# Expert phase: channel norm in 32x32 blocks turned by DVE, two batches ahead, in place of sixteen TensorE transpositions

## What is computed

```
out  = Wout @ attention(...) + b_out[:, None]            # per batch, 128 x 1024
mean = out.mean(axis=channels); var = out.var(axis=channels)
o    = (out - mean) * rsqrt(var + 1e-5) * g[:, None]     # channel norm: one mean, one variance per column n
x    = x + o
xf   = layernorm(x)                                      # over the 1024 columns of a row
scores = xf @ Wr.T                                       # 64 experts; top 16, softmax -> G
h    = xf @ A                                            # 64 x 16 = 1024 hidden values per row
x    = x + 2 * ((h * G) @ B)
```

## Time and profile before

| | |
|---|---|
| median of 3 runs | 2001.52 us (1999.25 to 2002.13) |
| profiled execution, its own time | 2002.66 us |
| its span in the profile | 2000.9 us |
| mean granted clock of TensorE | 0.99 |
| PE busy | 1920.2 us (96%), 10780 products |
| weight loads on PE | 1662.5 us (83%) |
| DVE busy | 1381.6 us (69%) |
| ACT busy | 1038.8 us (52%) |
| POOL busy | 803.9 us (40%) |
| DMA | 127.64 MB, mean 64 GB/s |

### The profile page before, as it was taken

How to read it: one execution, slowest core, us unless ns; L and a number is a source line. 1 busy time by engine, 2 the same in 40 slices (tenths; PEclk the granted TensorE clock), 3 DMA queues, 4 the chain that set the end, 5 groups by cost and what they waited for, 6 DMA issues and landing times. The chain is left out here.

```text
span 2000.9 us, 29856 instructions
## 1 busy us (share of the span) xinstructions
PE 1920.2 (96%) x10780; PEld 1662.5 (83%) x10780; DVE 1381.6 (69%) x1985; ACT 1038.8 (52%) x1303; POOL 803.9 (40%) x456
## 2 busy tenths in 40 slices
PE   4999999999999999999998699999999999999999
PEld 3778888888888888888886589999999999999998
DVE  5988888888888888888885654544444454444443
ACT  3888878787878787878785611111111111111111
POOL 3767676767676767667674000000000000000000
PEclk9999999999999999999999799999999999999999
DMA  3121111111111111212111611111111111111110
GB/s 117 44 72 61 68 63 63 63 63 63 63 63 65 61 73 52 73 52 73 52 43 37 213 61 64 63 57 46 54 63 63 63 63 63 63 63 51 44 41 32
DMA packets 43999, 127.64 MB, mean 64 GB/s; under 512 B 4224, under 2 KB 14080, under 8 KB 43968
## 3 DMA queue, kind: packets, MB, share of 16 engines
q1 hardware_dynamic: 39360, 110.44, 15.9%
q0 software_dynamic: 4608, 16.78, 2.7%
HBM read 93.65 MB, written 33.55 MB: 64 GB/s over the span
## 5 line engine op out<-in xcount | busy, mean ns | idle before, releaser
L282 POOL TENSOR_TENSOR kT_lo<-kT,kT_hi 128x1024 fp32r<-128x1024 f32 x128 | 304.4, 2399 | 0.6 <-ACT kT_hi L324 0.5
L278 POOL TENSOR_TENSOR eq<-eq,q_inv 128x1024 f32<-128x1024 f32 x128 | 242.4, 1904 | 140.6 <-DVE q_inv L499 140.6
L961 POOL TENSOR_TENSOR rstd_c<-var_c,minus_half 128x8 f32<-128x8 f32 x32 | 52.7, 1648 | 549.7 <-DVE var_c L1100 549.7
L52 PE MATMUL ps<-w_ra_hi,xT_hi 128*128 128x384 f32 (+1 forms) x768 | 257.9, 336 | 0.0
L54 PE MATMUL ps<-w_ra_hi,xT_lo 128*128 128x384 f32 (+1 forms) x768 | 252.2, 328 | 0.0
L53 PE MATMUL ps<-w_ra_lo,xT_hi 128*128 128x384 f32 (+1 forms) x768 | 251.9, 328 | 0.0
L983 ACT CAST hT_hi<-ps 128x512 fp32r<-128x512 f32 x64 | 37.7, 589 | 376.0 <-PE ps L1157 376.0
L52 PE MATMUL ps<-w_b_hi,hT_hi 128*128 128x512 f32 x512 | 205.7, 402 | 0.0
L342 ACT ACTIVATE ek<-ps,k_min 128x1024 f32<-128x1024 f32 x128 | 142.4, 1112 | 119.7 <-DVE k_min L503 119.7
L54 PE MATMUL ps<-w_b_hi,hT_lo 128*128 128x512 f32 x512 | 201.0, 393 | 0.0
L53 PE MATMUL ps<-w_b_lo,hT_hi 128*128 128x512 f32 x512 | 200.6, 392 | 0.0
(11 more groups left out here) (142 smaller groups left out, 4576.4 us busy)
## 6 DMA issues: line engine op xcount, KB each, us to landing
x_sb<-in_x SPq DMA_DIRECT2D x64, 512.0 KB, 4.1
ctx_sb<-in_ctx SPq DMA_DIRECT2D x32, 512.0 KB, 3.3
ctx_hi<-in_ctx POOLq DMA_DIRECT2D x32, 512.0 KB, 3.7
attention_out<-o_sb SPq DMA_DIRECT2D x32, 512.0 KB, 2.6
o_sb<-attention_out SPq DMA_DIRECT2D x32, 512.0 KB, 3.9
out<-out_sb SPq DMA_DIRECT2D x32, 512.0 KB, 2.9
x<-in_L_ffn_A SPq DMA_DIRECT2D x2, 512.0 KB, 4.0
o_sb<-in_L_ffn_A SPq DMA_DIRECT2D x2, 512.0 KB, 3.6
```

The lines of the kernel that those rows point to most:

```text
L52: pe.matmul(out, stat_hi, mov_hi, start=first, stop=False)
L278: pool.tensor_tensor(v, v, per_row(q_inv[:, i, :], 2 * HEADS, DH), ALU.mult).then_inc(q_normed, 1)
L282: pool.tensor_tensor(kT_lo[:, i % 2, :, :], kT[:, i % 2, :, :], kT_hi[:, i % 2, :, :].bitcast(F32), ALU.subtract).then_inc(kT_lo_ready, 1)
```

## The change

Steps now begin at t = -2, and the channel norm is made for batch u = t + 2 (`early`), in a different way:

- DVE turns o in 32x32 blocks from `o_sb` to `o_blk` (one instruction over 128x1024). In each block the 32 columns of o stand on partitions then, and the 32 channels along the row; the four bands of 32 partitions hold the four parts of the channels.
- ACT squares `o_blk` into PSUM slot 0, DVE sums each block's row of 32 (128x32 sums, `sq_part`).
- PE adds the four bands with one product of 32 columns by a constant matrix `row_mean` (1/128 where two partitions are alike modulo 32).
- DVE adds eps, POOL takes the power over 128x32, and then POOL, not DVE, multiplies `o_blk` in place by it.
- DVE turns the blocks back into `o_sb`. x2 reads it from there a step later.

PE's two turns of 8 transpositions each go, and hidden group 1 runs in one piece. The raw buffer that was half of `o_sb` is now `hg`; the loads of o are made two steps ahead of their use in x2; weight jobs are spread over steps -2, -1 and 0. On DVE the second block turn stands before the gating of the last hidden group, and on POOL the power for x2's rows stands before that for the channels. Cut to its core:

```diff
-            return {(-1, "var"): range(0, 2), (-1, "o"): range(2, 4), (-1, "y"): range(4, 6),
-                    (-1, "norm"): range(6, 7), (-1, "x"): range(7, A_JOBS),
+            return {(-2, "o"): range(0, 3), (-2, "y"): range(3, 5), (-1, "o"): range(5, 6),
+                    (-1, "y"): range(6, 7), (-1, "norm"): range(7, 8), (-1, "x"): range(8, A_JOBS),
 # SP
-                wait_for(sp, o_turned, b - 1)
+            def load_o(u, p):
+                wait_for(sp, x2_ready, u - 1)
+                sp.dma_start(o_sb[:, p, :], o_dram[u]).then_inc(o_loaded[p], 16)
-                    if n == 2:
-                        sp.wait_ge(o_stored[1], 16 * BATCHES // 2)
+                if not isinstance(t, int) or 0 < t + 2 < BATCHES:
+                    load_x(t + 2, par)
+                if not isinstance(t, int) or 1 < t + 3 < BATCHES:
+                    load_o(t + 3, 1 - par)
+            sp.wait_ge(o_stored[1], 16 * BATCHES // 2)
+            load_o(1, 1)
             load_weights()
 # POOL
                     pool.tensor_tensor(rstd[:, :], veps[:, :], w["minus_half"][:, :], ALU.pow).then_inc(rstd_ready, 1)
+                if early:
+                    pool.wait_ge(var_ready, u + 1)
+                    pool.tensor_tensor(rstd_c[:, :], var_c[:, :], w["minus_half"][:, 0:1].broadcast_to([P, NBLK]),
+                                       ALU.pow).then_inc(rstd_c_ready, 1)
+                    pool.wait_ge(rstd_c_ready, u + 1)
+                    v = o_blk[:, :].rearrange("p (n c) -> p n c", c=BLK)
+                    pool.tensor_tensor(v, v, per_row(rstd_c[:, :], NBLK, BLK), ALU.mult).then_inc(y_blocked, 1)
 # ACT
-                    act.activation(work[:, :], OT.rearrange(flat), ACT.Square).then_inc(squared, 1)
+                if early:
+                    act.wait_ge(o_blocked, u + 1)
+                    wait_for(act, x_lo_ready, u - 1)
+                    act.activation(SQ.rearrange(flat), o_blk[:, :], ACT.Square).then_inc(squared, 1)
 # DVE
+                if early:
+                    dve.wait_ge(o_loaded[par], 8 * (u - par) + 16)
+                    wait_for(dve, y_ready, u)
+                    dve.transpose(o_blk[:, :], o_sb[:, par, :]).then_inc(o_blocked, 1)
+                    dve.wait_ge(squared, u + 1)
+                    dve.tensor_reduce(sq_part[:, :], SQ.rearrange("p a (n c) -> p (a n) c", c=BLK), X,
+                                      ALU.add).then_inc(sq_summed, 1)
                 if mix:
                     top_scores(t)
                     gates(t)
                     gate_hidden(t, 0)
 ...
+                if early:
+                    dve.wait_ge(var_made, u + 1)
+                    dve.tensor_scalar(var_c[:, :], VAR, EPS, None, ALU.add).then_inc(var_ready, 1)
+                if mix:
+                    gate_hidden(t, 1)
 ...
                 if mix:
                     turned_hidden(t, 0)
+                if early:
+                    dve.wait_ge(y_blocked, u + 1)
+                    dve.transpose(o_sb[:, par, :], o_blk[:, :]).then_inc(y_ready, 1)
+                if mix:
                     gate_hidden(t, 2)
 # PE
-                    turn(OT.rearrange(flat), o_sb[:, p, :], o_turned)
+                if early:
+                    pe.wait_ge(sq_summed, u + 1)
+                    pe.matmul(VAR, row_mean[:, :], sq_part[:, :], start=True, stop=True).then_inc(var_made, 1)
-                    hidden(1, range(NCH // 2))
-                if ahead:
-                    pe.wait_ge(y_ready, b + 1)
-                    turn(YT.rearrange(flat), work[:, :], y_turned)
-                    hidden(1, range(NCH // 2, NCH)).then_inc(h_made, 1)
+                    hidden(1, range(NCH)).then_inc(h_made, 1)
```

More of the change, by code:

```diff
@@ L792 @@
 A_JOBS = 1 + KCH
+BLK = 32
+NBLK = N // BLK
 WEIGHT_JOBS = A_JOBS + KCH
@@ L814, in expert_mix @@
         work = sb("work", [P, N])
+        o_blk = sb("o_blk", [P, N])
+        row_mean = sb("row_mean", [P, P])
+        ident_sum = sb("ident_sum", [P, BLK])
         xT_hi = sb("xT_hi", [P, NCH, P], F32R)
@@ L836, in expert_mix @@
         gate = sb("gate", [P, EXPERTS])
-        raw = [x_sb[:, 1, :], x2[:, 1, :], o_sb[:, 1, :], out_sb[:, :]]
+        raw = [x_sb[:, 1, :], x2[:, 1, :], hg[:, :], out_sb[:, :]]
         RAW = len(raw)
@@ L893, in each_step @@
         def each_step(eng, step):
-            for t in (-1, 0, 1, 2):
-                step(t, t % 2, t >= 0, True, t >= 1)
-            with eng.Fori(0, (BATCHES - 4) // 2) as i:
+            for t in (-2, -1, 0, 1, 2):
+                step(t, t % 2, t >= 0, t >= -1, t >= 1, True)
+            with eng.Fori(0, (BATCHES - 6) // 2) as i:
                 for k in range(2):
-                    step(2 * i + 3 + k, (3 + k) % 2, True, True, True)
-            step(BATCHES - 1, (BATCHES - 1) % 2, True, False, True)
-            step(BATCHES, BATCHES % 2, False, False, True)
+                    step(2 * i + 3 + k, (3 + k) % 2, True, True, True, True)
+            for t in range(BATCHES - 3, BATCHES + 1):
+                step(t, t % 2, t < BATCHES, t < BATCHES - 1, True, t < BATCHES - 2)
         block = ctx.enter_context(nc.Block())
@@ L906, in _, with load_x @@
         def _(sp):
-            def load(b, p):
-                wait_for(sp, o_turned, b - 1)
-                if isinstance(b, int) and b == 1:
-                    sp.wait_ge(b_ordered[1], KCH // 2 - 1)
-                sp.dma_start(o_sb[:, p, :], o_dram[b]).then_inc(o_loaded[p], 16)
+            def load_o(u, p):
+                wait_for(sp, x2_ready, u - 1)
+                sp.dma_start(o_sb[:, p, :], o_dram[u]).then_inc(o_loaded[p], 16)
+            def load_x(b, p):
                 wait_for(sp, x2_ready, b - 1)
@@ L934, in load_weights, with step @@
                     sp.dma_start(dst, src).then_inc(raw_loaded[n % RAW], 16)
-            def step(t, par, mix, ahead, rest_):
-                if ahead and (not isinstance(t, int) or t + 2 < BATCHES):
-                    load(t + 2, par)
+            def step(t, par, mix, ahead, rest_, early):
+                if not isinstance(t, int) or 0 < t + 2 < BATCHES:
+                    load_x(t + 2, par)
+                if not isinstance(t, int) or 1 < t + 3 < BATCHES:
+                    load_o(t + 3, 1 - par)
                 if rest_:
@@ L941, in step @@
                     sp.dma_start(out[t - 1], out_sb[:, :]).then_inc(stored, 16)
+            sp.wait_ge(o_stored[1], 16 * BATCHES // 2)
+            load_o(1, 1)
             load_weights()
[L944 to L950, removed]
+            each_step(sp, step)
             sp.wait_ge(stored, 16 * BATCHES)
@@ L954, in _, with step @@
         def _(pool):
-            def step(t, par, mix, ahead, rest_):
+            def step(t, par, mix, ahead, rest_, early):
+                b, u = t + 1, t + 2
                 if ahead:
[L957 to L962, removed]
                     pool.wait_ge(veps_ready, b + 1)
@@ L983, in turned_hidden, with step @@
                 act.copy(dst, HT).then_inc(h_hi_ready, 1)
-            def step(t, par, mix, ahead, rest_):
-                b = t + 1
+            def step(t, par, mix, ahead, rest_, early):
+                b, u = t + 1, t + 2
                 weights(t, "start")
                 weights(t, "scores")
+                if early:
+                    act.wait_ge(o_blocked, u + 1)
+                    wait_for(act, x_lo_ready, u - 1)
+                    if isinstance(t, int) and t == 0:
+                        act.wait_ge(w_lo_ready, WEIGHT_JOBS)
+                    act.activation(SQ.rearrange(flat), o_blk[:, :], ACT.Square).then_inc(squared, 1)
+                weights(t, "o")
                 if mix:
@@ L1086, in gates, with step @@
                                   ALU.mult).then_inc(gates_ready, 1)
-            def step(t, par, mix, ahead, rest_):
-                b, p = t + 1, 1 - par
+            def step(t, par, mix, ahead, rest_, early):
+                b, p, u = t + 1, 1 - par, t + 2
+                if isinstance(t, int) and t == -2:
+                    dve.tensor_reduce(ident_sum[:, :], ident[:, :].rearrange("p (c j) -> p j c", j=BLK), X,
+                                      ALU.add).then_inc(ident_summed, 1)
+                    dve.wait_ge(ident_summed, 1)
+                    dve.tensor_scalar(row_mean[:, :].rearrange("p (c j) -> p c j", j=BLK),
+                                      ident_sum[:, :].unsqueeze(1).broadcast_to([P, P // BLK, BLK]), 1.0 / P, None,
+                                      ALU.mult).then_inc(row_mean_ready, 1)
@@ L1101, in step @@
-                weights(t, "var")
-                if mix:
-                    gates(t)
[L1104 to L1109, removed]
+                    gates(t)
                     gate_hidden(t, 0)
-                weights(t, "o")
@@ L1120, in step @@
                     wait_for(dve, added, b - 1)
-                    dve.scalar_tensor_tensor(out=x2[:, p, :], in0=YT.rearrange(flat), scalar=w["g"][:, 0:1],
```

(22 more changed lines are left out.)

28 lines of the change are left out of this document (12 added, 16 removed).

## The result

| | before | changed |
|---|---|---|
| median, us | 2000.69 (1999.25 to 2002.13, 4 runs) | 2102.36 (2102.11 to 2103.28, 4 runs) |
| ratio to before | | 1.0507, 95% interval 1.0494 to 1.0520 |
| span of the profiled execution, us | 2000.9 | 2100.1 |

The account below looks back on a forecast made before the run. PE, busy nearly all the span, was taken as the bound. 29 steps x (28.95 - 26.39) = 74.2, plus 17 beginning, minus 1.5 end, gave 89.7 on 2000.9, plus 0.6: 2091 us; range 2050 to 2120.

Parts of the forecast that it names:

- case A: Steady steps: the chain over POOL ends last and the clock falls in some steps; 2091 us, chance 0.56.
- POOL's power over 32 columns: Channel norm on POOL: 5.42 us, from a line through 546 ns for 1 column and 1648 ns for 8.
- The new chain: Each step, before PE's second-half turn: power 5.42, scaling 2.0, block turn 1.27, gating 0.56 to 0.6 us in a row.
- The cycle: One step, from PE's second-half turn round through addition, x2 and channel norm: 28.0 us instead of 26.39.
- PE's own work: PE's queue per step: two turns off (1.78 us), one 32-column product added (0.25), leaving 24.86 us.
- The clock: PE behind each 3.1 us stall: falls in half of the steps at 1.9 us, so 0.95 us a step.
- Rival B: Steady steps: same chain over POOL, but the clock never falls; 2064 us, chance 0.26.
- The beginning: Start of the expert phase: DVE's waits, extra block work and a later first load of A add 17 us.
- The end: Step 30 has neither turn nor chain, a gain of 1.5 us.
- Rival C: POOL's power isn't linear in its columns; at 1.65 us a step takes 24.9, the kernel 1965 us; chance 0.10.
- The even point: POOL's power time at which the changed kernel as a whole equals the one before: about 3.4 us.
- D: Block turn takes two passes, or the power 6.6 us: 1.2 us more each step, 2126 to 2137; chance 0.08.

Follow-up runs that it names:

- the first experiment: The changed kernel with POOL's power and scaling over only 8 of the 32 columns, leaving the norm wrong: 1971.76 us, ratio 0.9854.

## Why the prediction was right

The forecast was case A, and the time of 2102.36 us lies in its own range (2070 to 2120), 11 us above the value: 9.5 in the span, and the rest because the median is 2.3 above the profiled span where 0.6 was added. By its steps:

- **POOL's power over 32 columns**, the step on which the sign hung: 5.42 us from a line through two sizes, 5.436 measured. With 16 and 24 columns there are five sizes on one line, 157.5 ns a column from 8 to 32.
- **The new chain**: power, scaling, turn and gating put at 9.3 us, 9.20 measured. The block turn was put at 1.22 us from other passes, and is 1.23 to 1.25.
- **The cycle**: 28.0 put, 28.3 measured in steps without a fall. The 0.3 are before the power. From the turn behind the stall to the next first hidden group there are 4.67 us (4.56 put), the result products take 5.58 (5.50), the addition starts 0.29 behind them (0.2), and x2 starts 1.36 behind the addition (1.21; 1526.23 against 1524.87). Against that, from the small power to the power for the channels it is 0.51 (0.6).
- **PE's own work**: 24.86 put, 25.10 measured in the kernel with the turn moved. The timelines of both give the parts. The two turns took 0.8 each, and the late start of the product behind each, which I counted as 0.09 more, was not won: 24 result products take 5.58 us with no turn ahead of them, as with one. The added product takes 0.14 to the next one's start (I had 0.25), the hidden products of 384 columns from it to the next turn 6.42 against 2.11 + 4.26, and the three eighths of the result 4.28 against 4.21. So the gain in work is 1.30 us a step, not 1.53.
- **The clock**: falls in half of the steps at 1.9 us each were put, 0.95 a step; measured are 16 of 30 at 1.56 us, 0.83. The half was a guess between none and all that no row had picked, so that it came out near is luck. The price of 1.9 came from one fall at the kernel's start, where more products ran at the low level: a product of 512 columns starts 0.43 us behind the one before it there and 0.23 at the high level, so 1.56 us are eight such products. That fall was also read as the work of the 2.55 us stall before 40.13, and isn't: the level is 0.50 through all of 38 to 40 and 0.86 on the mean of 36 to 38, in which PE worked up to 37.6, so it was down when this stall began. Only two of the three falls among the four stalls were thus behind the stall named, and both were longer (3.71 and 5.14 us). The argument against B was weaker than it looked. Rival B (no fall) is out all the same; kept busy in the stall, the kernel takes 2076 us.
- **The beginning**: 17 us put, 19.0 measured. Of these 18.2 are there when PE starts on the turns of B (1147.63 against 1129.42 in the earlier trace rows). The sum is nearer than its terms. DVE's waits for POOL's scaling, put at some 6 and 4, are 5.1 and 2.7. The late first load of A, put at 2.5, is 2.4 late and worth 1.2 at most. Of the 6 of step -2, jobs put before the wait brought back 1.8. And PE stands 19.6 us in two waits (11.4 and 8.2) at the product with `row_mean`, the place at which the prediction put nothing.
- **The end**: 1.5 us of gain put, 0.5 of loss measured. One fall of 1.56 us in it, behind the last stall, makes most of that difference.

The sum was then 29 x 2.56 + 17 - 1.5 = 89.7, against 29 x 2.75 + 19.0 + 0.5 = 99.2. Of the 2.75 some 1.9 come from the chain alone (28.3 - 26.4), the rest from the clock.

Rival C, a power that isn't linear, is what the first experiment makes by force: I gave it a step of 24.9 and 1965 us, and it has 25.1 and 1972. The even point was put at a power of 3.4 us; 16 columns with 2.9 give 1998.3, just under the kernel before, and 24 with 4.2 give 2036.5, so it lies between the two, near 3.0 by a line through them. PE would have its lead back at 2.4 (2.9 less the wait of some 0.5), where I had put 2.3. Its mechanism was right and its condition was not met. Of D neither part held. What I called hidden stayed hidden: the product with `row_mean` waits for nothing in the steady part, and DVE's scores wait for PE as before. In the beginning it was not hidden, as said above.

What the prediction didn't see is how cheaply the loss could be avoided. It named what stood behind DVE's wait, and took this order as given. The y that DVE waits for is wanted a step later, the gating at once.

## What to carry to other kernels

Work taken off the engine that bounds a kernel is won only if that engine doesn't then wait for something that stands behind the new work in another engine's queue. The new work itself may have time to spare, as here. Where an engine works in strict order, put a wait for a long chain behind everything of that step that another engine wants now: here one instruction moved turned 5% slower into 1.2% faster. When an instruction's shape changes, price it by two sizes of itself, not by its count.

## What the runs showed of the hardware

- POOL's power -0.5 costs 157.5 ns for each column of 128 partitions, over some 390 ns, from 1 column (547 ns) to 32 (5436 ns). A multiplication over 128x1024 takes 1913 ns on the same engine, 1.87 ns a column: one column of power costs as much as some 84 of multiplication.
- TensorE's granted clock falls behind a stall that comes in each step, and how often depends steeply on its length, in one profiled execution of each kernel: in no step with waits up to 0.6 and up to 1.8 us, in 6 of 30 with 2.2 to 2.4, in 16 of 30 with 2.9 to 3.1 (the wait of step 0 is about a microsecond shorter in both, without a fall). Steps with the same wait differ, so the length is not all. The Trainium skill's page TensorE: Matmul & The Clock Gate, in the section Why this matters for your kernels, puts the limit at gaps of some 3 us; here it is a matter of share, and begins below that.
- PE kept at work in the stall keeps its clock, with f32 transpositions too: 26 of them left no step of 30 with a fall.
- DVE turns 128x1024 f32 values in 32x32 blocks in 1.24 us, no more than its other passes over this shape (1.21 to 1.28 us).
- The f32 product of 32 columns shows as two records, and the next product starts 0.14 us behind it.
